# A two-layer decoder on one Trainium2 core: one square sum to ScalarE, a root ahead of two convolutions, three GpSimdE steps and one ScalarE step later in the first stage

## What is computed

```python
q = short_conv(hidden_states @ Wq, wq_conv).reshape(B, T, H, DK)
k = short_conv(hidden_states @ Wk, wk_conv).reshape(B, T, NH, H, DK)
v = short_conv(hidden_states @ Wv, wv_conv).reshape(B, T, NH, H, DV)
q = l2norm(q)
k = l2norm(k)
beta = 2.0 * jax.nn.sigmoid(hidden_states @ Wb).reshape(B, T, NH, H)
g = -jnp.exp(A_log) * jax.nn.softplus(hidden_states @ Wa + dt_bias)
...
def step(S, x):
    q_t, k_t, v_t, b_t, g_t = x
    S = S * jnp.exp(g_t)[..., None, None]
    for i in range(NH):
        ki, vi, bi = (k_t[:, i], v_t[:, i], b_t[:, i])
        kv = jnp.einsum('bhk,bhkv->bhv', ki, S)
        S = S + bi[..., None, None] * jnp.einsum('bhk,bhv->bhkv', ki, vi - kv)
    o_t = jnp.einsum('bhk,bhkv->bhv', q_t, S)
    return (S, o_t)
```

## Time and profile before

| what | value |
|---|---|
| median of 3 runs | 2439.38 us |
| lowest and highest | 2432.64 and 2446.16 us |
| the profiled execution | 2436.64 us |
| its span, first to last instruction | 2434.8 us |
| busy of the span: PE, PEld | 90%, 75% |
| busy of the span: DVE, ACT, POOL | 64%, 49%, 30% |
| mean granted clock of PE | 0.956 of full speed |

### The profile page before, as it was taken

The page is one execution under the profiler, slowest core; times in us unless marked ns, Lnnn a source line. Parts: engine busy times, 40 slices in busy tenths (PEclk is TensorE's granted clock), DMA queues, the critical chain, the costliest instruction groups (busy, mean ns, idle before and its releaser), DMA issues. The chain is left out here.

```text
span 2434.8 us, 64577 instructions
## 1 busy us (share of the span) xinstructions
PE 2199.6 (90%) x27107; PEld 1826.6 (75%) x27107; DVE 1567.3 (64%) x3461; ACT 1182.7 (49%) x3272; POOL 722.4 (30%) x886
## 2 busy tenths in 40 slices
PE   5699999999989999837996899999986999999998
PEld 4578888887866888726885566667765888888887
DVE  5766667667544665566773666756667677777766
ACT  4545544554325777504553576756662333333332
POOL 3333334333324444324665434310110101101110
PEclk9899999999999999958998899999998999999999
DMA  4001100111103000022543200000000000000001
GB/s 147 22 11 37 37 28 11 37 37 34 37 3 116 19 15 15 19 79 67 125 96 70 62 2 2 2 2 2 2 9 14 21 25 27 21 27 27 20 7 35
DMA packets 87971, 83.50 MB, mean 34 GB/s; under 512 B 27265, under 2 KB 83457, under 8 KB 86273
## 3 DMA queue, kind: packets, MB, share of 16 engines
q1 hardware_dynamic: 81536, 70.98, 9.3%
q0 software_dynamic: 6144, 8.39, 2.0%
HBM read 68.71 MB, written 10.65 MB: 33 GB/s over the span
## 5 line engine op out<-in xcount | busy, mean ns | idle before, releaser
L2708 PE MATMUL bank<-f_XH,f_wp 128*128 128x512 f32 x1088 | 365.0, 397 | 5.9 <-DVE f_XL L2818 5.9
L2708 PEld LDWEIGHTS bank<-f_XH,f_wp 128*128 128x128 f32 x1088 | 208.9, 192 | 48.8 <-issue 5.0
L2708 PEld LDWEIGHTS bank<-f_wp,f_Hp 128*128 128x128 f32 x1632 | 215.0, 192 | 28.5 <-DVE X L2845 16.9
L2708 PE MATMUL bank<-f_wp,f_Hp 128*128 128x256 f32 x1632 | 219.2, 284 | 17.1 <-DVE X L2845 16.3
L2892 POOL TENSOR_TENSOR f_wp<-wa,f_wp 128x768 fp32r<-128x768 f32 x34 | 62.9, 1850 | 523.6 <-ACT f_wp L2858 523.6
L2708 PE MATMUL bank<-f_XL,f_wp 128*128 128x512 f32 x544 | 216.5, 398 | 0.0
L2843 DVE SCALAR_TENSOR_TENSOR X<-bank,f_w,X 128x256 f32<-128x256 f32 x512 | 211.4, 475 | 0.0
L799 DVE SCALAR_TENSOR_TENSOR a_acc<-a_praw,a_convw,a_acc 128x256 f32<-128x256 f32 x345 | 201.5, 591 | 9.4 <-ACT a_acc L946 1.2
L2881 ACT ACTIVATE f_Hp<-f_H 128x512 fp32r<-128x512 f32 x136 | 85.9, 632 | 225.9 <-DVE f_H L2830 225.9
L884 DVE COPY_PREDICATED wa<-masks,bank 128x512 f32<-128x512 uint8 x128 | 93.5, 732 | 111.7 <-PE bank L700 111.7
L2879 ACT ACTIVATE f_G<-bank 128x512 f32<-128x512 f32 x136 | 81.4, 598 | 165.9 <-PE bank L2708 165.9
(11 more groups left out here) (394 smaller groups left out, 5473.8 us busy)
## 6 DMA issues: line engine op xcount, KB each, us to landing
wa<-in_c_w SPq DMA_DIRECT2D x64, 256.0 KB, 3.3
wa<-in_f_gu SPq DMA_DIRECT2D x34, 256.0 KB, 2.8
wb<-grown SPq DMA_DIRECT2D x4, 1536.0 KB, 7.3
a_KQg<-grown SPq DMA_DIRECT2D x4, 1536.0 KB, 7.5
wa<-in_f_d SPq DMA_DIRECT2D x34, 128.0 KB, 2.8
a_E<-decays SPq DMA_DIRECT2D x16, 256.0 KB, 4.1
X<-in_x SPq DMA_DIRECT2D x4, 512.0 KB, 5.3
wa<-in_a_wqkv SPq DMA_DIRECT2D x1, 2048.0 KB, 9.1
```

Of the source, the lines that this page charges most:

```text
L2708: i = t.e.matmul(out_, lhsT[x], rhs[y], start=n == 0 and k == 0, stop=n == 2 and k == nk - 1, skip_group_check=True)
```

## The change

Five things change, all in stage A.
1. For block 0, the squares of the last of the four chunks are summed on ACT, as for the other blocks. DVE keeps three, and its three products have a place of their own each.
2. "root" of block 0 stands ahead of the taps of the third and fourth query tile, and of their projections; ACT's Exp ("edge" of block 0) stands behind the SiLU of the second query tile.
3. "grow" of chunk 0 goes from t = -2 to t = -1, that of chunk 1 from t = -2 to t = 0 (behind that of chunk 2).
4. "shift" of block 1 goes from t = -2 to t = -1.
5. "qs" of blocks 1 to 7 goes from slot 3 to slot 5 of its iteration.

```diff
-            order += silu0[4:8] + [conv0[8], ("kt", 0, 0), ("kt", 0, 1), conv0[9], ("sq", 0, 0), ("shift", 0), ("edge", 0), ("kt", 0, 2), ("sq", 0, 1)]
-            order += [("kt", 0, 3), ("sq", 0, 2), proj0[10], silu0[8], ("sq", 0, 3), ("root", 0), proj0[11], silu0[9], conv0[10], conv0[11]]
+            order += silu0[4:8] + [conv0[8], ("kt", 0, 0), ("kt", 0, 1), conv0[9], ("sq", 0, 0), ("shift", 0), ("kt", 0, 2), ("sq", 0, 1)]
+            order += [("kt", 0, 3), ("sq", 0, 2), ("sq", 0, 3), ("root", 0), proj0[10], silu0[8], proj0[11], silu0[9], conv0[10]]
+            order += [("edge", 0), conv0[11]]
...
-                                          (-4, 4, ("sq", 3)), (-4, 5, ("root",)), (-3, 0, ("small",)), (-3, 3, ("qs",)),
+                                          (-4, 4, ("sq", 3)), (-4, 5, ("root",)), (-3, 0, ("small",)), (-3, 5, ("qs",)),
...
-                    if (t - first) % 4 == 0 and 0 <= n < NB and step not in order:
+                    put = step in (("grow", 0, 0), ("grow", 0, 1), ("shift", 1))
+                    if (t - first) % 4 == 0 and 0 <= n < NB and step not in order and not put:
...
                     fill[1] += [("qs", 0)]
-                    fill[2] += [("grow", 0, 0)]
+                elif t == -1:
+                    fill[1] += [("grow", 0, 0)]
+                    fill[2] += [("shift", 1)]
+                elif t == 0:
+                    fill[1] += [("grow", 0, 1)]
...
-                    elif what == "sq" and s[1] == 0:
+                    elif what == "sq" and s[1] == 0 and s[2] < CB - 1:
...
-                        squares = Oc[:].rearrange("p c h d -> p (c h d)").rearrange("p (c h d) -> p c h d", c=2, h=H)[:, cc % 2]
-                        if cc > 1:
-                            v.wait_ge(squared.sem, squared.at[0, cc - 2])
+                        squares = (Oc[:, 0:2], Oc[:, 2:4], gt[:])[cc].rearrange("p c h d -> p (c h d)").rearrange("p (h d) -> p h d", h=H)
...
-                    elif what == "sq" and s[1]:
+                    elif what == "sq" and (s[1] or s[2] == CB - 1):
...
-                        if squared.at[n, cc] > 1:
+                        if n:
```

## The result

| | before | changed |
|---|---|---|
| median | 2436.68 us of 20 runs | 2430.80 us of 20 runs |
| lowest and highest | 2431.30 and 2446.34 us | 2424.89 and 2441.66 us |
| profiled execution, its span | 2436.64, 2434.8 us | 2441.57, 2439.4 us |
| mean granted clock | 0.956 | 0.948 |
| stage A's end: first matmul of the next stage on PE | 734.04 us | 731.07 us |

The ratio is 0.9976 (95%: 0.9965 to 0.9987): 5.9 us faster, where 15.4 us were forecast, and the median lies 6.8 us above the forecast of 2424.0. The gain is clear of the interval, but inside the 0.5% that the prediction calls hard to tell from none. Ratios further down are each to runs of the kernel before on the same chip.

The account below looks back on a forecast made before the run. TensorE, busy 90% of the span, was taken as the bound, so gains come from its idle or half-clock time in stage A. The terms sum to -15.4 us, giving a median of 2424.0 us (-0.63%), range 2413 to 2434.

Parts of the forecast that it names:

- Root, -1.2: Start of stage A, block 0: squares on ACT let the root start earlier on DVE; -1.2 us, between 0 and -1.3.
- Taps of t = -2, -5.8: In t = -2: DVE's taps run faster without POOL's growth and shift; -5.8 us, bounds nothing and -6.1.
- Clock behind those waits, -1.8: Behind TensorE's two start waits for DVE: full clock expected instead of 0.59; -1.8 us, between 0 and -1.8.
- t = -1, +0.5: POOL's moved steps hold taps in t = -1, mostly absorbed by DVE's idle time; +0.5 us, between 0 and +5.2.
- t = 0, +0.3: Growth of chunk 1 runs beside DVE's merge 877 in t = 0; +0.3 us, between 0 and +1.8.
- Block 1, -2.6: Query squares no longer delay ACT's copy of Y in t = 1: 1.2 us wait plus 1.45 us clock.
- Blocks 2 to 5, -4.4: Squares' move gains at most 1.1 us per block, DVE's chain being next, whether the clock recovers or not; -4.4 us.
- Blocks 6 and 7, -0.4: Squares' move gives 0 in block 6 and -0.4 us in block 7, which lacks projections (between 0 and -1.2).
- The later stages follow at a fixed distance: Stages after stage A keep their distance from its end, so its -15.4 us carries over to the whole time.
- half-clock stretches stay or only move: Rival, start and t = 1: the 1.8 and 1.45 us of clock are not gained; -12.2, 2427.2 us; chance 0.2.
- nothing of the query squares is gained beyond block 1: Rival, later blocks of stage A: DVE's chain is the bound in every block; +4.8, 2429 us; chance 0.1.
- The slower rival: POOL late with "xi" and decayed state in t = 0, DVE and TensorE wait; +3.7 us, 2443; chance 0.04.

Follow-up runs that it names:

- e7: The kernel before with only POOL's grow and shift steps moved later; one time, 2432.02 us.
- e4: The change itself, unedited, run again for a second profile; 2433.93 us, ratio 0.9989 of before.
- e1: The change without its fifth part, the query squares back in slot 3; 2433.32 us, 0.9986 of before.
- e9: The kernel before with DVE's "vt" put first in slot 5 and nothing else; 2433.65 us, ratio 0.9975 of before.
- e2: The kernel before with only the query squares moved from slot 3 to slot 5; 2438.75 us, ratio 1.0007 of before.
- e12: The kernel before, unedited, run again for a second profile; one time, 2440.53 us.
- e6: The kernel before with only the block 0 root parts (last squares on ACT, root ahead); one time, 2442.78 us.
- e3: The change with DVE's "vt" put ahead of the root's refinement and the weighing in slot 5; 2416.03 us, ratio 0.9911 of before.
- e10: The change with the root's refinement and the weighing one slot later, "vt" where it was; 2418.66 us, ratio 0.9906 of before.
- e11: The change with "vt" first, every block's shift and also its first growth one iteration later; 2410.44 us, ratio 0.9858 of before.
- e5: The change with "vt" first on DVE, but the query squares back in slot 3; 2425.17 us, ratio 0.9948 of before.
- e8: The change with "vt" first and the shift of every block one iteration later; 2409.05 us, ratio 0.9879 of before.

## Why the prediction was wrong in size

The terms are read on PE, at the starts of its kq, where the clock's part can be told from the rest: DVE's kq of t = -1, which the table has, already holds 0.8 us of the clock's gain.

- **Root, -1.2: right.** 1.17 and 0.78 us in the change's two profiles, 1.13 alone. The power starts at 63.30, forecast near 63.2.
- **Taps of t = -2, -5.8: right as the upper end.** DVE's taps gave what was counted, 5.20 and 0.60 us. On the path, PE's kq of t = -1 started at 98.20 before and starts at 92.00 and 91.63 in the change's two profiles; less the root that is 5.0 and 5.8 us, and 5.1 with POOL's steps alone (e7). What was late next was PE and its supply, as said, but it cost up to 0.8 us and not a tenth: 0.66 us of idle on DVE ahead of the X at 88.03. The two profiles with about 5.0 are those in which PE's granted clock was 0.50 from 71 to 79 us, ahead of that stretch; in e4 and e1, with 5.8, it was 1.00 there. The prediction also counts two waits of PE for DVE at the start. The same view has two more, 2.3 us for 879 at 76.57 and 1.2 us for 884; no term rests on them.
- **Clock behind those waits, -1.8: right.** The group from kq to the X behind it started at 98.20 and 102.06 before, 3.86 us, and at 92.00 and 94.11 now, 2.11 us, at 1.00 instead of about half.
- **t = -1, +0.5: right.** From that X to kq of t = 0 PE takes 0.6 us more than before, in the change, e4, e1 and e7 alike. The waits of 0.78 us for 888 and 0.48 for Y at 105.20 and 106.98, against 0.84 for Y before, are most of it. That the quarter of 2 us was the right share is luck: no row gave it, and the growth's hold of merge 881, 1.73 us for 0.43 without, was named but not priced.
- **t = 0, +0.3: nothing lost.** The merge takes 2.04 us beside the growth of 1.81 that started just ahead of it, as the Trainium skill (SBUF — State Buffer, section SBUF: two separate sides) has it for two-input instructions; the trace agrees on DVE. PE had other work: kq of t = 1 starts as early against before as that of t = 0, so the 1.8 us that this could have cost on the path were not paid.
- **Block 1, -2.6: right in size, half wrong in cause.** 2.67 us in the change and alone. But 1.45 of it, the clock, came in e1 and e7 too, with the wait of 2.00 still there, and in e9, whose kq of t = 1 is only 0.32 us early. So the clock's part does not need the squares' move, nor the earlier start; what decides it is open.
- **Blocks 2 to 5, -4.4: the step that failed.** It took 1.1 us a block as what DVE's chain leaves, "whether the clock recovers or not". The first part nearly held: against that of t = 5, PE's kq of t = 6 starts 0.86 us earlier in both profiles of the change (waits of 1.65 to 1.85 us for 866, expected up to 1.5, are what is left). The second did not. The clock was taken to be at stake only behind the wait for Y, and it moved with the wait: 3.64 us instead of 2.11 behind 866. A loss had no place in the term, though the start and the rival on the clock both spoke of half clock behind waits of about 2 us. The gain of DVE's kq from t = 5 to 9, 9 to 13, 13 to 17 and 17 to 21, that is by block:

| kernel | block 2 | block 3 | block 4 | block 5 |
|---|---|---|---|---|
| change | -0.69 | +0.86 | -0.69 | -0.65 |
| change again (e4) | +0.72 | +0.83 | -0.71 | -0.68 |
| query squares alone (e2) | +0.86 | +0.97 | -0.65 | -0.65 |
| before again (e12) | -0.05 | +1.62 | +1.52 | +0.06 |

  In block 2 the change and e4 are the same kernel with the same wait of 1.74 us; the one with half clock behind it loses 0.69, the one with full clock gains 0.72. In e2 that wait has full clock behind it too, and the gain is 0.86. Behind every other wait for "vt" in blocks 2 to 6 of these three kernels the clock fell. The gains in block 3 are owed to the first profile of before, which ran at half clock from 334 to 341 us and before again only to 338. In sum, from t = 2 to t = 21, the change loses 1.2 us, its second profile and e2 gain 0.1 each, where 4.4 were forecast. In the same stretch the kernels with the squares where they were gain 1.5 (e1), 3.7 (e7) and 3.2 us (e6 and e12) for no edit in it, so beside these single profiles the move costs something. e3 and e10, without the wait for 866, gain 11.2 and 13.6, more than the term held.
- **Blocks 6 and 7, -0.4: not settled.** From t = 21 to t = 29 the change loses 5.7 us (2.8 in its second profile), but before again loses 5.1 there too. So most of it is scatter. In the change's profile the waits of 1.65 and 2.26 us at 553.50 and 570.00 are each followed by half clock; behind the same 2.26 us the kernel before had 1.00 for the first 1.2 us.
- **"The later stages follow at a fixed distance": wrong by up to 8 us.** From stage A's end to the last instruction it was 1700.79 us before and 1708.34 in both profiles of the change; but no edit is there, and the other kernels lie between 1701.2 (e9) and 1708.6 (e11). It goes with PE's time at half clock in that part, from the granted clock of its trace: 148 us before, 152 in e9, 159 in e3, 179 in both profiles of the change, 176 in e5 and e8. Kernels with the squares' move stand at both ends (e2 1701.5, e8 1708.5), one without it at the upper (e5 1708.4). What sets it stays open. It took 7.5 us from the change's profile against that of before, and so perhaps a part from its median.

Of the rivals, "half-clock stretches stay or only move" is what happened, at another place than its condition: it took them to stay behind the waits of the start and of t = 1, where they went, and priced them as a gain not made (2427.2) rather than as a new cost. The rival that nothing of the query squares is gained beyond block 1 (2429) has the outcome right and lies within 2 us of the 2430.8 measured; its reason, DVE's chain, is half of it, and e3 and e10 show that the chain is a bound only through the order of DVE's steps. The sign "if the half clock returns elsewhere in the stage" came true. The slower rival did not occur: DVE waits for nothing of POOL in t = 0.

## What to carry to other kernels

When a wait on the bounding engine is removed, look at the next instruction that it waits for, and at what stands ahead of that one on its engine's in-order queue. Here 1.85 us of work that nobody waited for stood ahead of a copy that emptied a bank, and moving that copy up by a few positions made the edit worth about 9 us where it had been worth nothing. And a wait that moves can take its half-clock stretch along: 13 of the 15 waits for "vt" in the change's two profiles and in e2 were followed by one. Price the work behind the new wait at the lower clock too, when a wait of that length had it before.

## What the hardware showed that was not expected

- **A wait of one length, at one place, is followed by full or by half clock.** Behind the 2.00 us in t = 1 the clock was 0.63 before and 1.00 in e1. With 0.79 us at 219.96 alone it stayed at 1.00; after 1.74 more at 225.48 it was 0.54, and after the same two waits in the second profile of the same kernel 1.00.
- **Half clock without any wait.** In t = 6 PE has no idle time from 236.82 on, and at 240.61 runs the 16 matmuls of 128 x 1 that sum the query squares (1.95 us); behind them the clock falls. It does so in t = 10, 14 and 18 too. The windows of the changed kernel:

```profile
240.00:242.00 2.00, 2.00 (x37) 1.93 (x33) 1.97 (x2) 1.41 (x6) 2.00 (x2) 1.00 0.00 0
242.00:244.00 2.00, 2.00 (x31) 1.83 (x33) 1.93 (x4) 0.46 (x3) 1.08 (x2) 0.71 0.00 0
244.00:246.00 2.00, 2.00 (x32) 1.66 (x28) 1.97 (x5) 0.84 (x4) 0.99 (x2) 0.50 0.03 8
```

  The Trainium skill (TensorE: Matmul & The Clock Gate, What's actually happening) names idle time for the fall; here the trace shows a fall with no idle time of PE since the wait for "vt" at 225.48. The one-column matmuls alone are not the cause either: in e10 the same sixteen run in the same four iterations, and the clock stays at 1.00 behind each. In t = 6, with a later wait of 1.13 us for 858 in the window:

```profile
237.19:243.00 5.81, 4.68 (x88) 4.21 (x84) 5.67 (x10) 2.10 (x9) 3.89 (x5) 1.00 0.00 0
```

  What sets it off is open.
- **Two profiles of one kernel differ by up to 4.5 us at the end of stage A** (731.07 and 726.54), with 75.1 and 58.0 us at half clock in it. The half clock is where the two profiles differ; the waits from 110 to 630 us are nearly the same.
- **The held instruction need not be a long one.** Line 218, two small inputs from SBUF, took 0.41 us beside POOL's 1.04 us at 222.40, and 0.16 without. The merge with two SBUF inputs was held (1.73 and 2.04 us), the merge at 222.73, from a PSUM bank and inside that same step of POOL, was not (0.43).
